# Routed stage of a graph-attention and mixture-of-experts layer: expert weights copied into fixed places instead of addressed where they lie

## The reference, cut to what matters

```
gelu = lambda t: jax.nn.gelu(t, approximate=False)
shared = gelu(x @ W1s + b1s) @ W2s + b2s
rw = jax.nn.softmax(x @ Wr, axis=-1)
topw, topi = jax.lax.top_k(rw, K)                     # K = 2 of E = 8
topw = topw / jnp.sum(topw, axis=-1, keepdims=True)
mask = jnp.sum(jax.nn.one_hot(topi, E) * topw[..., None], axis=-2)
h = gelu(jnp.einsum('bsd,edf->bsef', x, W1p) + b1p)   # d = 128, f = 512
priv = jnp.einsum('bsef,efd->bsed', h, W2p) + b2p
routed = jnp.einsum('bsed,bse->bsd', priv, mask)
return shared + routed
```

## Time and profile before

| what | value |
|---|---|
| time, median of 3 runs | 1542.23 us (1539.29 to 1542.31) |
| time of the profiled execution | 1537.59 us |
| its span, first to last instruction | 1535.8 us |
| mean granted TensorE clock | 0.942 of full speed |
| routed stage, first DMA of SP to last scatter of POOL | about 943 to 1452 us |
| PE busy over the whole span | 80% |
| DVE, ACT, POOL busy over the whole span | 71%, 64%, 57% |
| mean busy share of the 16 DMA engines, 967 to 1355 us | 0.35 |

### The profile page before, as it was taken

How to read it: one execution, slowest core, us unless ns; L and a number is a source line. 1 busy time by engine, 2 the same in 40 slices (tenths; PEclk the granted TensorE clock), 3 DMA queues, 4 the chain that set the end, 5 groups by cost and what they waited for, 6 DMA issues and landing times. The chain is left out here.

```text
span 1535.8 us, 34679 instructions
## 1 busy us (share of the span) xinstructions
PE 1232.1 (80%) x9681; PEld 715.7 (47%) x9682; DVE 1094.9 (71%) x2538; ACT 984.0 (64%) x1785; POOL 873.4 (57%) x914
## 2 busy tenths in 40 slices
PE   2899999999999999955898996988898888877500
PEld 1566666666666666632344442433433433455300
DVE  3688988988888888855758773655565555555388
ACT  1677777777777777733677774877776777667400
POOL 3246666666666666645666762566665666655500
PEclk9999999999999999976999998999999999989855
DMA  2012211211222221112253432334333333223199
GB/s 60 29 56 65 67 61 62 69 64 58 68 69 69 69 69 55 42 46 78 87 148 115 129 98 57 65 75 80 72 82 69 77 74 79 59 55 55 33 339 315
DMA packets 219433, 127.34 MB, mean 83 GB/s; under 512 B 121903, under 2 KB 197726, under 8 KB 219372
## 3 DMA queue, kind: packets, MB, share of 16 engines
q1 hardware_dynamic: 185836, 84.39, 21.3%
q0 software_dynamic: 16896, 33.86, 6.8%
q10 hardware_dynamic: 16640, 8.39, 1.8%
HBM read 47.36 MB, written 54.04 MB: 66 GB/s over the span
## 5 line engine op out<-in xcount | busy, mean ns | idle before, releaser
L937 DVE SCALAR_TENSOR_TENSOR h<-hid,h 128x512 f16<-128x512 f32 (+1 forms) x448 | 282.4, 635 | 199.2 <-ACT h L917 158.6
L889 PE MATMUL Y<-h,w 128*128 128x512 f16 (+1 forms) x1344 | 295.7, 368 | 51.8 <-issue 34.7
L1254 POOL DMA_INDIRECT pairs_dram<-x_rows x272 | 280.0, 1029 | 87.9 <-issue 87.7
L917 ACT ACTIVATE h<-hid 128x512 f16<-128x512 f32 (+1 forms) x448 | 261.7, 584 | 65.7 <-PE Z L878 18.6
L928 ACT ACTIVATE hid<-Z,biases 128x512 f32<-128x512 f32 (+1 forms) x448 | 280.9, 627 | 0.0
L889 PEld LDWEIGHTS Y<-h,w 128*128 (+1 forms) x1344 | 130.9, 100 | 209.8 <-issue 106.2
L878 PE MATMUL Z<-x_rows,w 128*128 128x512 f16 (+1 forms) x960 | 201.8, 355 | 30.7 <-ACT hid L928 13.0
L421 DVE TENSOR_REDUCE smax<-S 128x8 f32<-128x1024 f32 x128 | 155.7, 1217 | 46.4 <-PE S L644 46.3
L1034 POOL DMA_INDIRECT slots_dram<-x_rows,pair_slot x140 | 142.9, 1020 | 71.9 <-issue 35.4
L424 DVE TENSOR_TENSOR probs<-S,smax 128x1024 f32<-128x1024 f32 x128 | 156.8, 1225 | 16.0 <-DVE smax L421 3.4
L557 ACT ACTIVATE probs<-probs 128x1024 f32<-128x1024 f32 x128 | 135.0, 1055 | 31.3 <-DVE probs L424 31.3
(11 more groups left out here) (181 smaller groups left out, 2090.5 us busy)
## 6 DMA issues: line engine op xcount, KB each, us to landing
y_pairs<-pairs_dram SPq DMA_DIRECT2D x32, 512.0 KB, 6.0
x_res<-in_x_dram SPq DMA_DIRECT2D x32, 256.0 KB, 3.1
adj<-in_adj_dram SPq DMA_DIRECT2D x32, 256.0 KB, 2.9
x_rows<-x SPq DMA_DIRECT2D x32, 256.0 KB
xT_dram<-xT SPq DMA_DIRECT2D x32, 256.0 KB
xTu<-xT_dram SPq DMA_DIRECT2D x32, 256.0 KB
out_dram<-x_res ACTq DMA_DIRECT2D x16, 512.0 KB, 7.9
pairs_dram<-x_rows POOLq DMA_INDIRECT x272
```

What stands on the lines that cost most here:

```text
L889: mm = pe.matmul(self.Yt[:, b, 0:w], self.w2[:, m, :, c][:, e, :], self.h16[:, b, k, c, 0:w], start=c == 0 and n == 0, stop=c == FC - 1 an ...
L917: act.activation(self.h16[:, b, 0, c, 0:w], self.hid[:, c, 0:w], ACT.Copy, scale=HS).then_inc(self.hi_done, 1)
L937: dve.scalar_tensor_tensor(out=self.h16[:, b, 1, c, 0:w], in0=self.hid[:, c, 0:w], scalar=HS, in1=self.h16[:, b, 0, c, 0:w], op0=ALU.mult, ...
L1254: pool.indirect_dma_start(pairs_dram, bass.IndirectOffsetOnAxis(ap=pair_of[n][:, j:j + 1], axis=0), y_sb[n % NY][:, j], None, bounds_check ...
```

## The change

The weights are laid out by expert, so that one expert's high and low parts of both matrices are 4096 bytes in a row in each partition (`weights`); `w1` and `w2` are views of it. In the routed stage eight places (`copies`) are set up in free SBUF, one for each input buffer. After its two DMAs for a unit, SP also loads the expert's number and starts a DMA that copies that expert's 512 KB from `weights` to the unit's place. PE waits for the rows and for the copy, and its matmuls name the fixed place. Its two loads of the expert's number per unit and the computed addresses are gone.

```diff
-        self.w1 = sb("w1", [P, 2, EA, F], F16)
-        self.w2 = sb("w2", [P, 2, EA, FC, P], F16)
+        self.weights = sb("weights", [P, EA, 4 * F], F16)
+        self.w1 = self.weights[:, :, 0:2 * F].rearrange("p e (k f) -> p k e f", k=2)
+        self.w2 = self.weights[:, :, 2 * F:4 * F].rearrange("p e (k c d) -> p k e c d", k=2, c=FC)
...
-                mm = pe.matmul(self.Z[:, c, 0:w], self.w1[:, k, :, c * P:(c + 1) * P][:, e, :], self.xT[:, b, m, 0:w],
+                mm = pe.matmul(self.Z[:, c, 0:w], w1[:, k, c * P:(c + 1) * P], self.xT[:, b, m, 0:w],
...
-                mm = pe.matmul(self.Yt[:, b, 0:w], self.w2[:, m, :, c][:, e, :], self.h16[:, b, k, c, 0:w],
+                mm = pe.matmul(self.Yt[:, b, 0:w], w2[:, m, c], self.h16[:, b, k, c, 0:w],
...
+    copies = [spare[:, at + n * 4 * F:at + (n + 1) * 4 * F] for n in range(NIN)]
+    w1 = [c[:, 0:2 * F].rearrange("p (k f) -> p k f", k=2) for c in copies]
+    w2 = [c[:, 2 * F:4 * F].rearrange("p (k c d) -> p k c d", k=2, c=FC) for c in copies]
+    copied = [sem(f"weights_copied{n}") for n in range(NIN)]
...
                 .then_inc(numbers_in[n], 16)
+            e = sp.value_load(unit_expert[0:1, bass.ds(u, 1)], min_val=0, max_val=E - 1)
+            sp.dma_start(copies[n].unsqueeze(1), f.weights[:, bass.ds(e, 1)]).then_inc(copied[n], 16)
...
-        def expert(u):
-            return pe.value_load(unit_expert[0:1, bass.ds(u, 1)], min_val=0, max_val=E - 1)
-
-        def unit(u, n, w, w1, w2):
+        def unit(u, n, w, wa, wb):
             pe.wait_ge(turned[n], turns(u, n, NIN) + 16)
-            f.hidden(pe, u, expert(u), n, w)
+            pe.wait_ge(copied[n], turns(u, n, NIN) + 16)
+            f.hidden(pe, u, w1[n], n, w)
             if not early(u, 1):
-                f.output(pe, u - 1, expert(u - 1), 1 - n % 2, w1)
+                f.output(pe, u - 1, w2[(n - 1) % NIN], 1 - n % 2, wa)
```

More of the change, by code:

```diff
@@ L869, in take_wait, with hidden @@
                            ALU.add).then_inc(self.took_wait, 1)
-    def hidden(self, pe, u, e, b, w=UT):
+    def hidden(self, pe, u, w1, b, w=UT):
         for c in range(FC):
@@ L877, in hidden, with output @@
             for n, (k, m) in enumerate(((0, 0), (0, 1), (1, 0))):
-                mm = pe.matmul(self.Z[:, c, 0:w], self.w1[:, k, :, c * P:(c + 1) * P][:, e, :], self.xT[:, b, m, 0:w],
+                mm = pe.matmul(self.Z[:, c, 0:w], w1[:, k, c * P:(c + 1) * P], self.xT[:, b, m, 0:w],
                                start=n == 0, stop=n == 2)
             mm.then_inc(self.z_ps, 1)
-    def output(self, pe, u, e, b, w=UT):
+    def output(self, pe, u, w2, b, w=UT):
         pe.wait_ge(self.lo_done, u * FC + FC)
@@ L1062, in unit @@
             pe.wait_ge(f.xT_ready[b], u * 8 + 16 if b == 0 else u * 8 + 8)
-            f.hidden(pe, u, SHARED, b)
+            f.hidden(pe, u, f.w1[:, :, SHARED], b)
             if not (isinstance(u, int) and u < 1):
-                f.output(pe, u - 1, SHARED, 1 - b)
+                f.output(pe, u - 1, f.w2[:, :, SHARED], 1 - b)
             if not (isinstance(u, int) and u < 2):
@@ L1076, in _ @@
         f.back(pe, U - 2, 0)
-        f.output(pe, U - 1, SHARED, 1)
+        f.output(pe, U - 1, f.w2[:, :, SHARED], 1)
         f.back(pe, U - 1, 1)
@@ L1206, in routed_phase @@
     pair_of = [spare[:, at + n * 2 * GT:at + (n + 1) * 2 * GT].bitcast(U32) for n in range(NIN)]
+    at += NIN * 2 * GT
+    copies = [spare[:, at + n * 4 * F:at + (n + 1) * 4 * F] for n in range(NIN)]
+    w1 = [c[:, 0:2 * F].rearrange("p (k f) -> p k f", k=2) for c in copies]
+    w2 = [c[:, 2 * F:4 * F].rearrange("p (k c d) -> p k c d", k=2, c=FC) for c in copies]
     slot_halves = slots_dram.bitcast(F16)
+    copied = [sem(f"weights_copied{n}") for n in range(NIN)]
     turned = [sem(f"rows_turned{n}") for n in range(NIN)]
@@ L1235, in _, with load @@
     def _(sp):
-        def load(u, n, w, w1, w2):
+        def load(u, n, w, wa, wb):
             if not early(u, LEAD):
@@ L1248, in _, with send @@
     def _(pool):
-        def send(u, n, w, w1, w2):
+        def send(u, n, w, wa, wb):
             pool.wait_ge(f.back_read, u + 1)
@@ L1265, in _ @@
     def _(pe):
-        def expert(u):
-            return pe.value_load(unit_expert[0:1, bass.ds(u, 1)], min_val=0, max_val=E - 1)
-        def unit(u, n, w, w1, w2):
+        def unit(u, n, w, wa, wb):
             pe.wait_ge(turned[n], turns(u, n, NIN) + 16)
-            f.hidden(pe, u, expert(u), n, w)
+            pe.wait_ge(copied[n], turns(u, n, NIN) + 16)
+            f.hidden(pe, u, w1[n], n, w)
             if not early(u, 1):
-                f.output(pe, u - 1, expert(u - 1), 1 - n % 2, w1)
+                f.output(pe, u - 1, w2[(n - 1) % NIN], 1 - n % 2, wa)
             if not early(u, 2):
-                f.back(pe, u - 2, n % 2, w2)
+                f.back(pe, u - 2, n % 2, wb)
         octets(pe, unit)
         f.back(pe, U - 2, 0, HALF)
-        f.output(pe, U - 1, expert(U - 1), 1, HALF)
+        f.output(pe, U - 1, w2[NIN - 1], 1, HALF)
         f.back(pe, U - 1, 1, HALF)
@@ L1306, in keep_yT, with unit @@
             f.keep_yT(dve, u, bass.ds(e, 1), b, w)
-        def unit(u, n, w, w1, w2):
+        def unit(u, n, w, wa, wb):
             f.lows(dve, u, n % 2, w)
             if not early(u, 1):
-                keep_yT(u - 1, 1 - n % 2, w1)
+                keep_yT(u - 1, 1 - n % 2, wa)
             if not early(u, 2):
-                keep_y(u - 2, n % NY, w2)
+                keep_y(u - 2, n % NY, wb)
         octets(dve, unit)
```

## The result

The changed kernel takes 1550.51 us (median of 15 runs, 1543.25 to 1561.21) against 1542.31 (15 runs, 1539.29 to 1553.03) for the one before on the same chip. The ratio is 1.0046 with a 95% interval from 1.0025 to 1.0066: slower by a little, where I had forecast 4% faster (1482 us).

A forecast was written before the change was run, and what follows sets the result against it. PE's 5.62 us pace was taken as the floor, with sequencer gaps making whole units 6.89 us. Sum: 1537.6 - 58.2 (whole units) - 4.6 (halves) + 2.7 (first unit) = 1477.5, plus 4.6 for the median: 1482 us, range 1464 to 1552.

The forecast's parts named there:

- I take it that the gaps of PE go for the most part: Whole units: with fewer PE sequencer instructions, units fall from 6.89 to 5.85 us, 58.2 us less.
- one unit in three: Whole units: about one in three was read as long, for example 9.11 us against an undisturbed 5.62 us.
- own range: Forecast without rivals: 1463 us with all gaps gone and halves at 3.7 us, to 1513 with gaps half gone.
- B: Whole units: stalls don't depend on PE's register instructions, so only the edges move; 1540 us, chance 0.14.
- C: Whole units: stalls come from DMA traffic and copies add to it, unit 7.50 us; 1575 us, chance 0.22.
- The halves: Half units: without PE's expert loads, 4.19 us falls to SP's 4.0 us, 4.6 us less; bounds 0 and 19.
- SP's turn of 4.00 us: SP's queue: with the added load and copy start, some 4.0 us per unit, just at a half's time.
- The first unit: Start of routed stage: PE's first matmul also waits for the first copy, 2.7 us more, once.
- The copies: Whole units: 512 KB copies raise the DMA share to 0.67, are not the bound, and cost nothing.
- A: Whole units: stalls come by PE's instruction count, 83 falling to 60 per unit; 1520 us, chance 0.12.

The follow-up runs named there:

- half-copy kernel: Changed kernel with only w1 copied (256 KB), the second layer reading the expert of its place: 1438.6 us, ratio 1.0009, on a quick chip.
- two products: Kernel before with 16 matmuls per unit in place of 24, low-half products left out, scatters kept: 1559.09 us, ratio 1.0041.
- third group: Repeats on a slow chip against the kernel before: changed kernel 1553.06 us, 1.006; fixed places without copies 1540.41, 0.9981; changed kernel with copy issued first 1546.95, 1.0024.
- direct writes: Kernel before with GpSimd's routed-stage scatters replaced by one plain SP DMA per unit: 1425.44 us, 0.9916 (quick chip); 1453.66 us, 0.937 (slow chip).
- fixed places and no copies: Changed kernel without SP's load and copy, PE using the first eight experts: 1551.57 us, 0.9972; again 1540.41, 0.9981; with plain writes replacing scatters 1424.43, 0.9908.
- least DMA: Kernel before with plain SP writes for scatters, and transposing and numbers' DMAs for the first eight units only: 1454.93 us, ratio 0.937.
- first group: Slow-chip runs of the change in parts, against the kernel before: unread copies added 1.0104; fixed places without copies 0.9972; 64-byte copy 0.9975; later transposing DMAs dropped 0.9903.
- copies beside: Changed kernel's layout, load and 512 KB copies, but PE addresses experts where they lie and waits for no copy: 1570.55 us, ratio 1.0104.

## Why the prediction was wrong

**The step that failed** is "I take it that the gaps of PE go for the most part". It took 58.2 us off the sum. The runs give 0.2 to 0.3% for it, 3 to 4 us (0.9972 [0.9946, 0.9997] and 0.9981 [0.9955, 1.0008], the second not told from nothing), and in the changed kernel the register instructions are short while a whole unit takes 7.13 us. The register instructions are slow in long units, but other engines stand still then too, and the same instructions take 46 to 51 ns once GpSimd's scatters are gone. I read a symptom as the cause, and the sign against it was in the rows that I had: SP's DMA starts scattered from 17 to 2104 ns for one kind, on an engine whose program has nothing to do with TensorE's addresses. In the changed kernel's trace this is still so, and in the half-copy kernel's on a quick chip it is not (nor on a slow chip without scatters, where the transposing DMA's start takes 1212 to 1687 ns):

```profile
L1251 SPq DMA_DIRECT2D x_rows<-weights x80: 4/553/1396, 950.4 to 1450.5; - x80
```

```profile
L1251 SPq DMA_DIRECT2D x_rows<-weights x80: 542/558/621, 923.2 to 1332.6; - x80
```

One reading was wrong beside this. I took one unit in three to be long. By the starts of PE's transposes 32 of 55 take over 6 us, so a gap is what most units have. And that 1550.5 us lies within the 1464 to 1552 that I gave is no merit of the forecast, whose own range ended at 1513: the upper part came from B and C.

**What holds in its place.** On a slow chip the whole units are long where GpSimd scatters in them. This was shown on one chip, in two kernels, by putting plain writes of SP in place of the scatters (5.54 us for each unit). The edit takes away the indirect addressing, GpSimd's part and the order of the rows together, and which of them counts it does not say. On the same chip the kernel with two products keeps the scatters and takes 7.18 us a unit. Of the 6.3% of the whole time 0.8% come on a quick chip too, without a long unit, so some 5.5% are the long units' own. The kernel before has them in two traces from slow chips and needs about the same time on all three. On the two quick ones no traced kernel had them, scatters or not; the kernel before left no trace there.

**The halves.** Forecast 4.6 us less, measured none (4.05 and 4.06 us; 4.03 and 4.15 in the third group). The forecast started from 4.19, the mean of 21 halves; from 4.05 to 4.0 it would have been 1 us. SP's turn of 4.00 us was right. That PE could go faster without its address work was not: on a quick chip, with direct writes, a half takes 3.95 us with fixed places and no copies, and (1342.0 - 1251.6) / 23 = 3.93 with computed addresses. Nor is it SP that holds these two up, since with the least DMA a half takes (1372.1 - 1280.8) / 23 = 3.97.

**The first unit.** Forecast +2.7 us. SP's first load starts at 942.5 us in the kernel before and the first transposes of PE at 963.6, 21.1 us later; in the changed kernel 946.6 and 970.2, 23.6 us. So +2.5 us, about as worked out. The changed kernel's wait:

```profile
953.84 2.72 PE L879 MATMUL Z<-x_rows 128*128 128x512 f16 x6 [8.22 <-DMA x_rows<-weights]
```

**The copies.** Costed at nothing. They cost 1.0104 [1.0064, 1.0144] beside computed addresses, and with fixed places 1.0046 or 1.006 against 0.9972 to 0.9981 for the kernels without the bytes: 0.7 to 0.8%, some 11 us, of which the first unit has 2.5. By the traces of the first group most of the rest lies in the whole units, 7.55 us with copies beside and 7.18 without. Where units are not long, the copies leave them so: 5.55 us with half copies and scatters, (1250.8 - 945.2) / 55 = 5.56 with full copies and direct writes. Full copies with scatters were not run there. So the bytes have no price of their own in such a stage, and on slow chips they come on top of stalls that are there anyway. How they make them worse was not shown.

**The rivals.** A (count of instructions) is refuted: PE has 60 instructions per unit instead of 83, and 29 of 55 units are over 6 us from one set of transposes to the next where 32 were, and units of the kernel with direct writes have all 83 and are never long. Instructions are not being fetched either. DMA packets of the changed kernel from 1080 to 1240 us, where the unit above (14.1 us) and two others of 11.9 and 13.4 us lie:

```profile
DMA packets 40832, 23.12 MB, mean 145 GB/s; under 512 B 36608, under 2 KB 36608, under 8 KB 40832
...
q1 hardware_dynamic: 38016, 17.35, 41.0%
q0 software_dynamic: 2816, 5.77, 11.2%
```

The queues of instructions (q8 and q14 on the profile's page) have no row in these 160 us, though the loop goes round more than twice, and the same stretch of the kernel before has none either, with a loop of 8 x 83 = 664 instructions on PE. The Trainium skill ("Runtime: NRT & Kernel Launch", section "Instruction fetch mechanics") says that the instruction memory is refilled in blocks as a program runs on and that a taken branch can force a fetch; by this trace a loop of eight units, once entered, goes round without a fetch. B (the stalls don't ask about PE's registers) came nearest, 1540 us against 1550.5, and had the right reason; I gave it 0.14. C (traffic) had the right sign. Its cause is refuted in its general form. Left without the transposing DMAs, at 101 packets a us, the units stay long, and with direct writes on a slow chip there is not one long unit at 101387 / 273 = 371 packets a us. DMA packets of that kernel from 967 to 1240 us:

```profile
DMA packets 101387, 25.40 MB, mean 93 GB/s; under 512 B 76800, under 2 KB 101376, under 8 KB 101376
```

In the narrow form, that copies add to stalls which the scatters make, C stands.

**What stays open.** What in a scatter holds up SP, PE and ACT, why on some chips only, and whether fewer scatters per unit would do, since the runs for that fell on a chip without stalls. No version that computes the reference beat the kernel before: the direct writes leave the rows unsorted, and moving the sorting into the last stage was not tried. The kernel before and the changed one were not timed against each other on a quick chip.

## What to carry to other kernels

Before costing a slow instruction as removable, look whether the same kind is slow at the same moments on an engine that has nothing to do with it; if it is, take the trigger away, not the victim. A cheap experiment that removes the suspected work entirely (here fixed places without copies) belongs ahead of a change that replaces it with other work. And an issuing queue has a period of its own: count its DMAs per unit (here 4.0 us for three, 5.36 for four) before adding one.

## What the runs showed of the hardware

From one chip to another, each used once, the time differs by far more than the change did: the same kernel takes 1438 us on two of the five and 1542 to 1553 on three. The kernel with direct writes was traced on one of either kind and moves the same 246823 packets on both. It takes 1425.44 and 1453.66 us, and 27 of these 28 us lie before the routed stage: SP's first load in it is at 917.6 us on the quick chip and at 944.5 on the slow one. What costs them was not looked into. Long gaps have a second price: after TensorE had stood 3.67 and 1.99 us, with three matmuls between, it ran at the granted clock 0.50 for the next 5 us. And with a third of its matmuls left out, the stage ran at clock 0.87 and no faster.
